# Six tiles' top-54 masks, residual sums and small factors on GpSimd in a two-layer attention and expert kernel

## What is computed

```
x += softmax(mask(ln(x) @ ctx.T / 16)) @ ctx                      # block 1, attention
x += sum over the 2 best of 8 experts of w * (silu(h@Wg)*(h@Wu))@Wd   # block 2, h = ln(x)
s  = coef * (ln(x) @ Wq.T) @ ctx.T                                # block 3
thr = 54th largest of each row of s
x += (softmax of s where s >= thr, 0 elsewhere) @ ctx @ Wo.T
h  = ln(x); q = round(h * 127/max|h|)                             # block 4, rounded factors
g  = gelu((q @ sign1) * scales)
x += (round(g * 127/max|g|) @ sign2) * scales
```

## Time and profile before

| | us |
|---|---|
| median of 3 runs | 443.55 (442.79 to 444.75) |
| profiled execution | 437.4 |
| its span, first to last instruction | 435.7 |
| DVE busy / PE busy / ACT busy / POOL busy in the span | 299.9 / 353.8 / 181.5 / 49.4 |

### The profile page before, as it was taken

The page is one execution under the profiler, slowest core; times in us unless marked ns, Lnnn a source line. Parts: engine busy times, 40 slices in busy tenths (PEclk is TensorE's granted clock), DMA queues, the critical chain, the costliest instruction groups (busy, mean ns, idle before and its releaser), DMA issues.

```text
span 435.7 us, 6602 instructions
## 1 busy us (share of the span) xinstructions
PE 353.8 (81%) x2075; PEld 282.1 (65%) x2082; DVE 299.9 (69%) x760; ACT 181.5 (42%) x312; POOL 49.4 (11%) x100
## 2 busy tenths in 40 slices
PE   0899999999899996089898989878968872656984
PEld 0466777777799895047578988766655561625863
DVE  2432445762311024537999999999999999999983
ACT  2062353442534233024337255437656610443485
POOL 4100000115000001760000000170100000000010
PEclk9999999999999999559999999989998995969899
DMA  7583886609478992845878996453450031413301
GB/s 251 178 260 116 296 301 215 185 25 346 146 230 265 308 292 90 251 160 188 249 229 265 294 326 202 153 157 121 118 185 14 0 118 46 116 35 105 114 15 48
DMA packets 70809, 76.38 MB, mean 175 GB/s; under 512 B 5356, under 2 KB 69496, under 8 KB 70776
## 3 DMA queue, kind: packets, MB, share of 16 engines
q1 hardware_dynamic: 57272, 59.93, 44.0%
q10 hardware_dynamic: 11968, 11.84, 8.3%
q0 software_dynamic: 1536, 4.20, 2.9%
HBM read 66.91 MB, written 9.04 MB: 174 GB/s over the span
## 4 chain that ended last, share of the span: by engine, by line
PE 43%; DVE 31%; issue 13%; DMA 7%; ACT 2%; POOL 1%; SPq 1%; ACTq 0%; DVEq 0%; POOLq 0%
PE S L868 13%; PE GU L946 9%; DVE fold L1233 6%; DVE cand_h L1221 6%; PE A L895 6%; DVE cand_l L1228 5%; PE O L956 4%; DVE fold L1238 3%; PE A L899 3%; PE T L882 3%; DMA xg<-xs 2%; DMA v_sb<-ctx 2%; DVE row L1261 2%; DMA x_res<-x 2%; DVE gabs L1327 2%
## 5 line engine op out<-in xcount | busy, mean ns | idle before, releaser
L637 ACT ACTIVATE pT<-T 128x512 f32<-128x512 f32 x64 | 31.4, 514 | 79.0 <-PE T L882 74.9
L899 PE MATMUL A<-pT,v_sb 128*128 128x128 f32 (+1 forms) x416 | 54.1, 287 | 8.1 <-ACT pT L637 4.7
L946 PE MATMUL GU<-xgT,wg_ring 128*128 128x128 f32 x480 | 58.6, 276 | 2.1 <-DVE hid L1160 1.1
L946 PEld LDWEIGHTS GU<-xgT,wg_ring 128*128 128x128 f32 x480 | 56.9, 192 | 4.3 <-issue 1.9
L899 PEld LDWEIGHTS A<-pT,v_sb 128*128 128x128 f32 (+1 forms) x416 | 51.6, 202 | 10.9 <-issue 6.6
L1221 DVE MAX8 cand_h<-fold 128x8 f32<-128x801 f32 x56 | 55.0, 991 | 0.0
L868 PE MATMUL S<-k_sb,qT 128*128 128x400 f32 (+2 forms) x128 | 47.6, 518 | 4.4 <-ACT qT L694 1.3
L895 PE MATMUL A<-v_sb,pT 128*128 128x256 f32 (+1 forms) x208 | 49.6, 381 | 0.9 <-DMA v_sb<-ctx 0.9
L868 PE MATMUL S<-k_sb,xT 128*128 128x400 f32 (+2 forms) x128 | 48.5, 515 | 0.8 <-ACT xT L622 0.8
L1233 DVE MATCH_REPLACE8 fold<-cand_h,fold 128x801 f32<-128x801 f32 x48 | 47.1, 984 | 0.0
L895 PEld LDWEIGHTS A<-v_sb,pT 128*128 128x128 f32 (+1 forms) x208 | 37.9, 190 | 7.7 <-DMA v_sb<-ctx 1.5
(11 more groups left out here) (153 smaller groups left out, 488.4 us busy)
## 6 DMA issues: line engine op xcount, KB each, us to landing
v_sb<-ctx SPq DMA_DIRECT2D x36, 512.0 KB, 4.2
wg_ring<-Wg SPq DMA_DIRECT2D x30, 256.0 KB
wg_ring<-Wu SPq DMA_DIRECT2D x30, 256.0 KB
wd_ring<-Wd SPq DMA_DIRECT2D x30, 256.0 KB
k_sb<-ctxT SPq DMA_DIRECT2D x16, 400.0 KB, 5.4
xg<-xs ACTq DMA_DIRECT2D x30, 128.0 KB, 3.8
ys<-y_sb ACTq DMA_DIRECT2D x30, 128.0 KB, 3.5
k_sb<-ctxT SPq DMA_DIRECT2D x8, 402.0 KB, 4.2
```

The costliest lines, as they stand in the source:

```text
L637: act.activation(pT[0:r, i % NPT, :, :].rearrange("p a s -> p (a s)")[:, 0:w], t_bank("pT", *key)[0:r, 0:w], ACT.Copy).then_inc(pTe_done, 1)
L899: mm = pe.matmul(A_bank[:, o * P:(o + 1) * P], v[0:r, a, o * P:(o + 1) * P], pT[0:r, j, a, :], start=m == 0 and o == 0, stop=m == NMC - 1 ...
L946: mm = pe.matmul(gu_bank(*key)[:, a * F + f * P:a * F + (f + 1) * P], wg_ring[:, w % NWG, a, k, f * P:(f + 1) * P], cols[:, k, :], start=k ...
```

## The change

For tiles 0 to 5 (`CUT_POOL`, `SUM_POOL`) three of DVE's steps are split in two:
- `cut` becomes, in four pieces of up to 512 columns, `ge` (row >= thr, to 1 or 0, in place) and `cutp` (times the exponential) on POOL, and `psum` on ACT, one pass over the masked row for its sum. PE's `pT` of a piece waits for its `cutp`; `pairH`/`pairL` and `exp3` of tile t+2 and `rc3` wait for `psum`.
- `x3` becomes `x3a` on ACT (PSUM times scale into `xn4`) and `x3p` on POOL (add to `x_res`).
- `fin` becomes `fina` on ACT and `finp` on POOL.

For all eight tiles `va4`, `cent`, `xmx`, `xscl`, `xdeq` and `gdeq` move from DVE to POOL, with the same arithmetic. The whole `ORDER` is written anew, 1473 steps where there were 1413. The step list is too long to show; here is the new one where `pairH.0` is led up to,

The code:

```diff
...
@@ -404,6 +412,13 @@
...
             return GU_bank[GU_USE[("GU", *step)] % 2]
+        def row_cut(eng, t):
+            if t in CUT_POOL:
+                eng.wait_ge(psum_done, n("psum", t))
+            else:
+                eng.wait_ge(cut_done, n("cut", t, CUTS[t][-1]))
 
...
@@ -584,10 +599,64 @@
...
                         .then_inc(yg_in[i % NYG], 16)
+                elif op == "ge":
+                    t, u = key
+                    m0, m1 = 4 * P * u, min(M, 4 * P * u + 4 * P)
+                    pool.wait_ge(thr_done, n("thr", t))
+                    pool.wait_ge(exp3_done, n("exp3", t))
+                    pool.tensor_scalar(p_row(t)[:, m0:m1], row3[:, t % 4, m0:m1], thr3[:, t:t + 1], None, ALU.is_ge) \
+                        .then_inc(ge_done, 1)
+                elif op == "cutp":
+                    t, u = key
+                    m0, m1 = 4 * P * u, min(M, 4 * P * u + 4 * P)
+                    pool.wait_ge(ge_done, n("ge", t, u))
+                    pool.wait_ge(exp3_done, n("exp3", t))
+                    pool.tensor_tensor(p_row(t)[:, m0:m1], p_row(t)[:, m0:m1], e_row(t)[:, m0:m1], ALU.mult) \
+                        .then_inc(cutp_done, 1)
                 elif op == "rs4":
...
                     pool.tensor_tensor(rstd4[:, t:t + 1], var4[:, t:t + 1], minus_half[:, 0:1], ALU.pow).then_inc(rs4_done, 1)
+                elif op == "x3p":
+                    t = key[0]
+                    pool.wait_ge(x3a_done, n("x3a", t))
+                    pool.wait_ge(norm_done, n("norm", 3, ROW_OF[t]))
+                    pool.tensor_tensor(x_res[:, t, :], xn4[:, t % 2, :], x_res[:, t, :], ALU.add).then_inc(x3p_done, 1)
+                elif op == "finp":
+                    t = key[0]
+                    pool.wait_ge(fina_done, n("fina", t))
+                    pool.tensor_tensor(fin[:, t % 2, :], fin[:, t % 2, :], x_res[:, t, :], ALU.add).then_inc(finp_done, 1)
+                elif op == "gdeq":
+                    t = key[0]
+                    pool.wait_ge(gmx_done, n("gmx", t))
+                    pool.wait_ge(wqb_done, 2)
+                    pool.tensor_tensor(gdeq[:, t:t + 1], gmx[:, t:t + 1], wdeq[:, 1:2], ALU.mult).then_inc(gdeq_done, 1)
+                elif op == "va4":
+                    t = key[0]
+                    pool.wait_ge(ag4_done, n("ag4", t))
+                    pool.tensor_scalar(var4[:, t:t + 1], mv4[:, t, 1:2], EPS, None, ALU.add).then_inc(va4_done, 1)
+                elif op == "xdeq":
+                    t = key[0]
+                    pool.wait_ge(xmx_done, n("xmx", t))
+                    pool.wait_ge(wqb_done, 1)
+                    pool.tensor_scalar(xdeq[:, t:t + 1], xmx[:, t:t + 1], wdeq[:, 0:1], 1.0 / 127.0, ALU.mult, ALU.mult).then_inc(xdeq_done, 1)
+                elif op == "xscl":
+                    t = key[0]
+                    pool.wait_ge(xinv_done, n("xinv", t))
+                    pool.tensor_scalar(xscl[:, t:t + 1], xinv[:, t:t + 1], rstd4[:, t:t + 1], 127.0, ALU.mult, ALU.mult).then_inc(xscl_done, 1)
+                elif op == "xmx":
+                    t = key[0]
+                    pool.wait_ge(xabs_done, n("xabs", t))
+                    pool.wait_ge(rs4_done, n("rs4", t))
+                    pool.tensor_scalar(xmx[:, t:t + 1], xabs[:, t:t + 1], rstd4[:, t:t + 1], EPS, ALU.mult, ALU.max) \
+                       .then_inc(xmx_done, 1)
+                elif op == "cent":
+                    t = key[0]
+                    pool.wait_ge(ag4_done, n("ag4", t))
+                    if t >= 2:
+                        pool.wait_ge(q4_done, n("q4", t - 2))
+                    pool.tensor_scalar(xn4[:, t % 2, :], x_res[:, t, :], mv4[:, t, 0:1], None, ALU.subtract) \
+                       .then_inc(cent_done, 1)
 
...
@@ -710,11 +779,16 @@
...
                         if t - 2 >= EARLY:
-                            act.wait_ge(cut_done, n("cut", t - 2, CUTS[t - 2][-1]))
+                            row_cut(act, t - 2)
                     else:
...
                        .then_inc(exp3_done, 1)
+                elif op == "psum":
+                    t = key[0]
+                    act.wait_ge(cutp_done, n("cutp", t, NU - 1))
+                    act.activation(e_row(t)[:, 0:M], p_row(t)[:, 0:M], ACT.Copy, accum_out=sum3[:, t, 0:1]) \
+                       .then_inc(psum_done, 1)
                 elif op == "aTe":
...
@@ -722,6 +796,20 @@
...
                        .then_inc(aTe_done, 1)
+                elif op == "x3a":
+                    t = key[0]
+                    act.wait_ge(wo_done, n("wo", t))
+                    act.wait_ge(rc3_done, n("rc3", t))
+                    if t >= 2:
+                        act.wait_ge(q4_done, n("q4", t - 2))
+                    act.activation(xn4[:, t % 2, :], O_bank[:, 0:D], ACT.Copy, scale=r3[:, t:t + 1]).then_inc(x3a_done, 1)
+                elif op == "fina":
+                    t = key[0]
+                    act.wait_ge(dn_done, n("dn", t))
+                    act.wait_ge(gdeq_done, n("gdeq", t))
+                    if t >= 2:
+                        act.wait_ge(stored[t % 2], 16 * (t // 2))
+                    act.activation(fin[:, t % 2, :], O_bank[:, 0:D], ACT.Copy, scale=gdeq[:, t:t + 1]).then_inc(fina_done, 1)
                 elif op == "xmul":
...
@@ -825,9 +913,9 @@
...
                 elif op == "wo":
-                    pe.wait_ge(x3_done, n("x3", *key))
+                    pe.wait_ge(x3a_done if key[0] in SUM_POOL else x3_done, n("x3a" if key[0] in SUM_POOL else "x3", *key))
                 else:
-                    pe.wait_ge(fin_done, n("fin", *key))
+                    pe.wait_ge(fina_done if key[0] in SUM_POOL else fin_done, n("fina" if key[0] in SUM_POOL else "fin", *key))
 
...
@@ -875,7 +963,10 @@
...
                     else:
-                        pe.wait_ge(cut_done, n("cut", t, u if len(CUTS[t]) > 1 else 0))
+                        if t in CUT_POOL:
+                            pe.wait_ge(cutp_done, n("cutp", t, u))
+                        else:
+                            pe.wait_ge(cut_done, n("cut", t, u if len(CUTS[t]) > 1 else 0))
                         src = p_row(t)
...
@@ -1206,7 +1297,7 @@
...
                     if t >= 2:
-                        dve.wait_ge(cut_done, n("cut", t - 2, CUTS[t - 2][-1]))
+                        row_cut(dve, t - 2)
                     row, f = row3[:, t % 4, :], fold[:, t % 2, :]
...
@@ -1263,8 +1354,11 @@
...
                     t = key[0]
-                    dve.wait_ge(cut_done, max(n("cut", t, u) for u in CUTS[t]))
-                    if len(CUTS[t]) > 1:
+                    if t in CUT_POOL:
+                        dve.wait_ge(psum_done, n("psum", t))
+                    else:
+                        dve.wait_ge(cut_done, max(n("cut", t, u) for u in CUTS[t]))
+                    if t not in CUT_POOL and len(CUTS[t]) > 1:
                         link(dve.tensor_reduce(sum3t[:, t:t + 1], sum3[:, t, :], AX.X, ALU.add))
...
@@ -1278,49 +1372,21 @@
...
-                    dve.wait_ge(x3_done, n("x3", t))
+                    dve.wait_ge(x3p_done if t in SUM_POOL else x3_done, n("x3p" if t in SUM_POOL else "x3", t))
...
-                elif op == "va4":
-                    t = key[0]
-                    dve.wait_ge(ag4_done, n("ag4", t))
-                    dve.tensor_scalar(var4[:, t:t + 1], mv4[:, t, 1:2], EPS, None, ALU.add).then_inc(va4_done, 1)
-                elif op == "cent":
-                    t = key[0]
-                    dve.wait_ge(ag4_done, n("ag4", t))
-                    if t >= 2:
-                        dve.wait_ge(q4_done, n("q4", t - 2))
-                    dve.tensor_scalar(xn4[:, t % 2, :], x_res[:, t, :], mv4[:, t, 0:1], None, ALU.subtract) \
-                       .then_inc(cent_done, 1)
...
-                elif op == "xmx":
-                    t = key[0]
-                    dve.wait_ge(xabs_done, n("xabs", t))
-                    dve.wait_ge(rs4_done, n("rs4", t))
-                    dve.tensor_scalar(xmx[:, t:t + 1], xabs[:, t:t + 1], rstd4[:, t:t + 1], EPS, ALU.mult, ALU.max) \
-                       .then_inc(xmx_done, 1)
...
-                elif op == "xscl":
-                    t = key[0]
-                    dve.wait_ge(xinv_done, n("xinv", t))
-                    dve.scalar_tensor_tensor(out=xscl[:, t:t + 1], in0=xinv[:, t:t + 1], scalar=127.0,
-                                             in1=rstd4[:, t:t + 1], op0=ALU.mult, op1=ALU.mult).then_inc(xscl_done, 1)
-                elif op == "xdeq":
-                    t = key[0]
-                    dve.wait_ge(xmx_done, n("xmx", t))
-                    dve.wait_ge(wqb_done, 1)
-                    dve.scalar_tensor_tensor(out=xdeq[:, t:t + 1], in0=xmx[:, t:t + 1], scalar=1.0 / 127.0,
-                                             in1=wdeq[:, 0:1], op0=ALU.mult, op1=ALU.mult).then_inc(xdeq_done, 1)
...
```

217 lines of the change are left out of this document (110 added, 107 removed).

## The result

The changed kernel takes 446.37 us at the median of 15 runs (441.87 to 449.39), the kernel before 441.24 (437.40 to 444.75, 15 runs) beside it: a ratio of 1.0124, with an interval of 1.0093 to 1.0156. It is slower by 1.2% (5.1 us between the medians), where 430.5 and a gain of 3% were forecast, with a range of 422 to 440.

What follows compares the result with a forecast made beforehand. DVE was taken to bound the kernel from the first pairH to thr.7. Terms -17 (DVE work), +3 (waits), +0.7 (tail), +0.3 (front) gave -13 off the 443.55 us median: 430.5, forecast 427 to 433.5, range 422 to 440.

Steps and rivals of the forecast that it cites:

- The front: Stretch up to pairH.0: reordered first layers, router steps and early expert tiles together cost +0.3 us (-3 to +4).
- PE's clock: In the front: PE, busy beforehand, should be granted more than 0.64, shortening qT.0 and the first four s3 (7.26).
- signs of being wrong: DVE idle above 8 us in the stretch, POOL pieces above 2, or pairH.0 moved from 198.7 by more than 4.
- DVE's busy sum: Over the whole span: DVE's busy sum falls by about 27 us, POOL's rises from 49 to near 110.
- The waits: Between pairH.0 and thr.7: DVE waiting for results of POOL costs 3 us in all (0 to 8).
- The size of a mask: On POOL per masked tile: ge 0.9 and cutp 1.3 per piece, 6.9 us a tile, bounds 3.8 to 10.7.
- DVE's own work: Between pairH.0 and thr.7: net 19.1 us of steps removed, 16.0 after overlaps; 17 taken off.
- The tail: Behind thr.7: small factors in series on POOL add 0.9, less work ahead gives 0 to -2; +0.7 us (-2 to +3).
- (a): Rival, search stretch: POOL's reads and DVE's two-input instructions hold each other up, 5 us, time 435.5; chance 0.14.
- (c): Rival: long POOL masks stall DVE at pairH.2, pairH.3, pairH.6, pairL.7; 4.7 us, time 435, 456 at worst; chance 0.08.
- (d): Rival: the change does little since a worse front or tail eats it, time 443; chance 0.05.
- (b): Rival: PE becomes the bound until the experts are through, gain shrinks by 3 to 4 us, time 434; chance 0.12.

Runs made afterwards that it cites:

- e15: Changed kernel with group 0's expert steps 8 to 14 back in old order and group 1's routing and scatters moved later; ratio 1.0174 to the kernel before.
- e18: e15 without group 1's eight scatters (part of the computation left out), its weight loads held until group 0's last down product; ratio 1.0009 to the kernel before.
- e9: Changed kernel with only group 0's expert steps 8 to 14 back in the old order among themselves; ratio 1.0129 to the kernel before.
- e3b: Changed kernel with two weight loads one place earlier and group 1's weight loads held until group 0's last down product; ratio 1.0089 to the kernel before.
- e1: Code of the kernel before in the new step order, none of the work moved; ratio 1.0357 to the kernel before.
- e2: Code of the kernel before with the new order only up to the first pairH, the old order behind it; ratio 1.0183 to the kernel before.
- e13: Kernel before, old order, with sums and small factors moved, masks left on DVE, order behind thr.7 untouched; ratio 1.0120 to the kernel before.
- e14: Changed kernel with steps that made DVE wait in the search put further back, order behind thr.7 left alone; ratio 1.0264 to the kernel before.

## Why the prediction was wrong

**The front is the step that failed.** The prediction gave it "+0.3 (-3 to +4)"; it measured +9.8. Its terms were that `router.3` and `rank.1` come "before the last `down.0`, about 1.2 more in front of the gathers", and some 2 for expert tiles ahead of `qT.0`. It priced the router steps by their own length. What counts is who is queued behind them: `down.0.9` on PE and SP's load behind that, then the last experts' weights, and at the end of e15 to e18 `mul.0.14` on DVE. The experts' own order cost 1.5 us at the last y store (e9), routing and scatters together 3.0 (e15), and another 3.2 arise where e15 to e18 leave the routing ahead of the last `down.0`. It also followed none of the DMA steps which the order moves past each other: the prefetched weights beside the y store cost 2 to 3 (e3b, e18). And it took PE's clock for a gain only; in the whole stretch it is, 0.78 for 0.64, but it fell under the last experts' products and cost 2.7 there. These parts are measured one on top of another and partly hold the same microseconds, so they aren't to be added; that the whole is the order's is what e1 and e2 show. The part behind the gather went as forecast or better: 23.4 from the first gather to `pairH.0`, 26.2 before. Two of the three signs of being wrong that the prediction named came true: `pairH.0` moved by more than 4, and DVE idled more than 8 in the stretch. The third, POOL pieces above 2, did not (one `ge` of 18, 2.56). DVE's busy sum fell by 19.8 where about 27 was forecast, and POOL's rose to 130 for 110.

**The waits are the second.** "3 in all (0 to 8)", measured +10.4 of idle time. At `pairH.2` the terms can be read one by one. Forecast: 11.9 from `thr.0` to the end of `psum.0`, 13.8 of DVE steps. Measured (timeline of ACT in the changed kernel):

```profile
239.79 1.28 ACT L785 ACT_TABLE_LOAD   x1
241.08 1.63 ACT L785 ACTIVATE fold<-row,nmax 128x1601 f32<-128x1601 f32 x1
...
252.26 1.54 ACT L790 ACTIVATE fold<-row 128x1601 f32<-128x1601 f32 x1 [2.10 <-POOL row L614]
253.71 0.19 ACT L790 ACTIVATION_READ_ACCUMULATOR fold<-row 128x1 f32 x1
```

`thr.0` is at 235.38, so the table load came 4.4 later, as ACT's queue had score copies, an expert's `silu` and a y copy ahead of it that waited for PE; the prediction had let it start at once. From the exponential's end to `psum` it is 9.55, where the mask was taken as 6.9. The room was 14.5. Hence 4.04. Without the 4.4 in ACT's queue, `psum.0` would have ended 14.1 behind `thr.0` and DVE would not have waited, even with the mask as long as it was: the term that failed at `pairH.2` is the queue's, which had been put at nothing. The size of a mask is the second term: `ge` 1.62 and `cutp` 1.28 for 512 columns give 1.62 x 3 + 0.46 + 1.28 x 3 + 0.33 = 9.5 a tile, against 0.9 and 1.3 and 6.9. It lay inside the bounds (3.8 to 10.7), and I should have gone by the upper one, since `ge` reads a scalar through a pointer as no POOL row before did. `cent`, the same kind of instruction, took 0.96 against 0.3 to 0.6.

**DVE's own work** fell by 13.0, where 17 was taken and 16.0 had come out. Counted without overlaps, the masks gave 10.8 (11.3 forecast), `x3` 2.5 (2.9), `cent` 1.3 (1.8) and `mul` 1.2 (1.7). The small steps (0.15 in the record) gave back about 0.06 each and `xmx` 0.14, since they overlap both neighbours in the record; and `pairH` and `pairL` count 0.8 more in all, about half of it because more of them stand behind a wait, where no earlier step overlaps them.

**The tail** was +0.7 (-2 to +3) and measured +1.5. POOL's serial chain is there, 1.27 at `xabs.7` and 0.59 at `xinv.7`, but e1, without it, has a tail of 32.3: in the new order the move adds nothing. In the old order it does, 34.2 in e13 for 30.3.

**The rivals.** (a), contention, is real and small: where `pairH` meets a mask piece it takes 1.40 (0.99 alone) and the piece 2.56 (1.57), but the mean of the eight `pairH` is 1.04, and the other fifteen pair steps are as fast as alone. With one small step (0.62 for 0.17, at 316.15) DVE lost 0.9 us by it in all. That such a pair contends is what the Trainium skill (SBUF — State Buffer, Who interferes with whom) says; the trace agrees, with both sides lengthened. (c), the latency of the mask, is not borne out as it was written: at `pairH.2` the mask as measured would just have fitted, and the wait of 4.04 comes of what stood ahead of `exp3.0` on ACT. At `pairH.3`, `pairH.6` and `pairL.7`, the other places that (c) named, at most 0.5 was lost. The sign was turned by the order, and mostly by its front, which had been (d)'s "a worse front or tail eats it", with a chance of 0.05 and a time of 443. (b), PE's busy time as the next bound, isn't shown (73.56 of 81.4 us in its stretch, 76.40 of 81.3 before). What it is akin to is the chain through group 1's experts, y stores and gathers, which sets tile 4's scores, so that a faster DVE only arrives there earlier.

Undoing the new order while keeping the moved work would settle whether the work alone is a gain. I did not manage an order for that: my hand-made ones lose more in waits than the work gives. The nearest is e13, which moves the sums and small factors alone and loses 1.2%. What the runs show is that within the new order the moved work is worth 2.3%, and that the new order, without it, costs 3.6%.

## What to carry to other kernels

When a change comes with a new order, price the order first and as a whole: an order that is remade moves every queue, and a step of 1 us ahead of products and loads costs what is queued behind it; routing steps priced at 1.2 in all were, with their scatters, worth 3 at the last y store, and not all of their cost was taken away. A kernel of the old code with the new order is the first run to make, since it tells in one go which part is the order's. And when work leaves a full engine, ask for the next chain that sets the same point: here the gathers of group 1 were due 13 us later, and of 4.4 us that e14 saved on DVE ahead of tile 4, 1.9 were left at its first pair step.

## What the runs showed of the hardware

On POOL a one-input `TENSOR_SCALAR` with a pointer scalar is slower than a two-input `TENSOR_TENSOR` of the same width: 1.62 against 1.28 us for 512 columns, 0.96 against 0.73 for 256. The Trainium skill (GPSIMD Engine Reference, 3.1 Elementwise — side-by-side cycle accounting), cited in the prediction, gives 769 ns as its best case for 512 elements, which the prediction took for one input, half of what was measured; its two-input figure, 1.12 by proportion, is near the 1.28. The measurement decides. Small factors of one column cost 0.18 to 0.39 on POOL, and up to 1.10 where one met a DVE pair step (`xscl` at 283.26).
